# Attention and routed FFN: the slot rows' fill as eleven transfers beside the score tiles in place of four in a row

## The chip, the cores and the metric

The kernel runs on one core of a Trainium2 chip. A core has a matmul engine (TensorE, PE; its weight load is PEld), VectorE (DVE), ScalarE (ACT), GpSimd (POOL), SyncE (SP), which does nothing here but issue DMA transfers, and 16 DMA engines that all queues share. The metric is the device time of one execution in microseconds (us), taken as the median of several runs. A profile of one more execution gives the trace that is read below.

## The reference

Four sequences of 1024 rows of width 128 go through four residual blocks, each behind a layer norm:

```
x = x + attention_a(layernorm(x))      # 8 heads of 128, softmax(Q K^T + relative positions) V
x = x + ffn(layernorm(x))              # 8 experts, top 2 of each row
x = x + attention_b(layernorm(x))      # 16 heads of 8, causal
x = x + ffn(layernorm(x))

attn_pos = relative_shift(einsum(Q + rel_pos_bias, rel_k))   # row i of the product shifted by i
a = softmax(attn + attn_pos);  out = einsum(a, V) @ w_out + b_out

h = x W1[e]^T + b1[e];  g = h[:256] * sigmoid(h[256:])
out += (g Wo^T + bo) * share[e]         # for the two experts of each row
```

All is fp32. The weights and products that need it are split into a high and a low part, and a product is three matmuls.

## The kernel before

**Order of the work.** Three lists of steps (plans) are made in Python, and each engine walks through the same list and emits its share of each step. Plan 0 is attention_a, which takes about the first 1,600 us; plan 1 is the first FFN and attention_b; plan 2 the last FFN. What follows here is plan 0 (`plan_a`, from line 113).

**The score tiles.** The 256 tiles (4 sequences x 8 heads x 8 tiles of 128 query rows) are numbered 0 to 255, and step s of the plan works on tile s. Four tiles are a group (qd), 64 groups in all. For the relative positions, a strip of the position product is made three tiles ahead: TensorE multiplies (L1049, L1050), ScalarE and VectorE copy the result to `a_rt` (L1361 and L1798), SyncE stores it to DRAM (`rout`, L698, scr<-a_rt, 576 KB) and reads it back two tiles ahead with a row stride that is one element short, which makes the shift (`rin`, L707, a_sp<-scr, 512 KB). `a_rt` has two buffers, so ScalarE's copy for tile t waits for the store of tile t - 2 to have landed; the store and the load of neighbouring tiles are issued one behind the other. Then VectorE adds the scores of tile s to the strip and finds the maximum (L1806; one per tile, it waits for the load and for TensorE's L478 to L480), ScalarE takes the exponential (L1369), TensorE transposes (L1075), ScalarE and VectorE split the result (L1376, L1812), and TensorE multiplies by V (L1088 to L1090). When a group's product is done, ScalarE copies it out (L1382, a_osh) and raises the semaphore `o_hi` by one; group qd is copied in step 4 qd + 8.

**The slot rows.** The FFN is routed. Each row of x is scattered to the slots of its two experts in three arrays in DRAM, `xsd[0..2]`, one for each part of the sequences, with 39, 23 and 23 tiles of 128 rows (`PT[0]`). Slots that no row takes must hold finite numbers, so all the arrays are first filled with rows of the input q. This is the fill: DRAM to DRAM, issued by POOL (L785), 5.57 MB in all, in four transfers of 2048, 448, 1472 and 1472 KB. It is counted on the semaphore `d_zero`, together with the load of the output bias `fbo` (L787).

**POOL's list.** POOL runs its code in this order: the constants at the start; the expert weights W1 one by one (`w1` steps of the plan, at s = 52, 54, ... 68: L773 and L632 load 256 and 254 KB to SBUF, L781 subtracts, ScalarE and VectorE split the result, the semaphore `w1_lo` counts them); the fill; then, behind a wait for the last `w1_lo`, `fbo` and four constants (L788 to L794) that the ranking matmuls use; then the scatters of the first two parts (`m_disp`, L850), of which the first waits for `d_zero`. VectorE's `m_bias` step waits for `d_zero` too.

Of the kernel before, what the change touches and what calls it, by code (L numbers as in the profile page):

```python
# [16 lines left out]
B, L, D = 4, 1024, 128  # L17
# [25 lines left out]
PT = [[2 * L // 128 * len(p) + E - 1 for p in parts] for parts in PARTS]  # L43
PG = [[(t + 3) // 4 for t in row] for row in PT]
PP = [[(t + 1) // 2 for t in row] for row in PT]
MT = PT[0][0] + 1

ROWS = list(range(NT)), [n for k in range(8) for n in (3 * k, 3 * k + 1, 3 * k + 2, 24 + k)]
SC = float(DK) ** -0.5
# [438 lines left out]
class Program:  # L488
# [269 lines left out]
    def gpsimd(self, e):  # L758
        S = self.S
        cond = dict(pattern=[[-1, 128]], channel_multiplier=1, base=0)  # L760
        e.memset(self.ident[:, :], 0.0).then_inc(S["const"], 1)
        e.wait_ge(S["const"], 1)
        e.affine_select(out=self.ident[:, :], in_=self.ident[:, :], compare_op=ALU.not_equal, fill=1.0,
                        **cond).then_inc(S["const"], 1)
        e.iota(self.iota[:, :], pattern=[[1, E]], base=0, channel_multiplier=0,
               allow_small_or_imprecise_dtypes=True).then_inc(S["const"], 1)
        w1 = self.dr["w1t"].rearrange("d (e h) -> d e h", e=E)
        e.wait_ge(S["prod_mm"], H)
        for k in range(-1, E):
            if k > 0:  # L770
                e.wait_ge(S["w1_lo"], k)
            if k + 1 < E:
                e.dma_start(self.w1st[:, (k + 1) % 2, :], w1[:, k + 1, :]).then_inc(self.d_w1[(k + 1) % 2], 16)  # L773
                self.bottom_row(e, self.w1r[:, (k + 1) % 2, :], "w1r", self.d_w1[(k + 1) % 2], slice(512 * k + 512, 512 * k + 1024))
            else:
                e.dma_start(self.w1st[:, 0, 0:256].rearrange("p (k d) -> p k d", k=2),
                            self.dr["wo_f"].rearrange("(k p) d -> p k d", p=128)).then_inc(S["d_wo"], 16)
            if k >= 0:
                st = self.w1st[:, k % 2, :]
                e.wait_ge(self.d_w1[k % 2], 48 * (k // 2 + 1))  # L780
                e.tensor_tensor(st, st, self.w1r[:, k % 2, :], ALU.subtract).then_inc(S["w1_sub"], 1)  # L781

        for i, n0, n in ((0, 0, B * L), (0, B * L, PT[0][0] * 128 - B * L), (1, 0, PT[0][1] * 128), (2, 0, PT[0][2] * 128)):
            e.dma_start(self.xsd[i][n0:n0 + n, :], self.dr["q"][0:n, :]).then_inc(S["d_zero"], 16)  # L785
        e.wait_ge(S["w1_lo"], E + 1)
        e.dma_start(self.fbo[:, :], bass.AP(self.dr["bo_f"].tensor, 0, [[0, 128], [1, 128]])).then_inc(S["d_zero"], 16)  # L787
        e.memset(self.ones[:, :], 1.0).then_inc(S["m_const"], 1)  # L788
        e.wait_ge(S["m_const"], 1)
        e.affine_select(out=self.upper[:, :], in_=self.ones[:, :], compare_op=ALU.is_gt, fill=0.0, pattern=[[1, 128]],  # L790
                        channel_multiplier=-1, base=0).then_inc(S["m_const"], 1)
        e.iota(self.tio[:, :], pattern=[[1, MT]], base=0, channel_multiplier=0,
               allow_small_or_imprecise_dtypes=True).then_inc(S["m_const"], 1)
        e.iota(self.j128[:, :], pattern=[[128, 16]], base=0, channel_multiplier=0,  # L794
               allow_small_or_imprecise_dtypes=True).then_inc(S["m_const"], 1)
        for u in self.plans[0]:
            if u[0] == "m_disp":
                self.gpsimd_routed(e, u)

        self.first_attention_done(e)  # L800
        nst = 0
        for u in self.plans[1]:
            if u[0] == "b_s":
                _, b, g, ch, J, q = u
                pt, nst = nst % NP, nst + 1
                if J >= 4 * ch:
                    off = 128 * (J - 4 * ch)
                    e.wait_ge(S["b_exp"], nst)
                    e.affine_select(out=self.P[:, pt, off:off + 128], in_=self.P[:, pt, off:off + 128],  # L809
                                    compare_op=ALU.is_ge, fill=0.0, pattern=[[1, 128]], channel_multiplier=-1,  # L810
                                    base=0).then_inc(S["b_masked"], 1)
            elif u[0] == "b_load":
                dr = self.dr
                e.dma_start(self.pst, dr["w_b"].rearrange("d (k n) -> d k n", k=6)).then_inc(S["d_wb"], 16)
                e.dma_start(self.wvst[:, :], dr["wv_b"]).then_inc(S["d_wb"], 16)
                e.dma_start(self.bq[:, :], dr["bias_b"]).then_inc(S["d_wb"], 16)
                e.dma_start(self.bvo[:, :], bass.AP(dr["bvo_b"].tensor, 0, [[0, 128], [1, 136]])).then_inc(S["d_wb"], 16)
                e.memset(self.maskq[:, :], 0.0).then_inc(S["const"], 1)
                e.wait_ge(S["const"], 4)
                e.affine_select(out=self.maskq[:, 384:512], in_=self.maskq[:, 384:512], compare_op=ALU.is_ge, fill=NEG,  # L820
                                **cond).then_inc(S["const"], 1)
            elif u[0] == "b_zero":
                if u[1]:
                    e.wait_ge(S["m_ftr"], NT)
                    e.wait_ge(S["m_pmm"], NT)
                e.memset(self.K[u[1]][:, :, :].bitcast(F32), 0.0).then_inc(S["const"], 1)
            else:
                self.gpsimd_routed(e, u)
        for u in self.plans[2]:
            self.gpsimd_routed(e, u)  # L830

    def gpsimd_routed(self, e, u):
        S = self.S
        if u[0] == "m_disp":
            _, f, n = u
            i, part = 24 * f + n, part_of(f, n)
            if i == 0:
                e.wait_ge(S["d_zero"], 80)
            if n == 8 * PARTS[f][part][0]:
                e.wait_ge(S["m_slot"], 3 * f + part + 1)  # L840
                if f:
                    e.wait_ge(S["m_tr"], at(PG, 0, part + 1))
            if part == 2:
                rows, sem = self.xn8[:, n - 24, :], self.d_scat_last
                e.wait_ge(S["ln_xn"], 2 * ln_rank(2 * f + 1, B - 1) + 2)
            else:
                rows, sem = self.xd[:, i % 2, :], self.d_scat[i % 2]
                e.wait_ge(S["m_xd"], i + 1)
            for k in range(2):
                e.indirect_dma_start(self.xsd[part], bass.IndirectOffsetOnAxis(self.slot[:, k, n:n + 1], 0), rows,  # L850
                                     None).then_inc(sem, 16)
        elif u[0] == "m_gath":
            _, f, n = u
            i, part = NT * f + n, part_of(f, n)
            if n == 8 * PARTS[f][part][0]:
                end = at(PP, f, part + 1)
                for p in range(end - 4, end):
                    e.wait_ge(self.d_gs[p % 4], 16 * (p // 4 + 1))
            if i == 0:
                e.wait_ge(S["b_wlo"], 1)  # L860
            if i >= NP:
                e.wait_ge(S["m_sum"], rank(*divmod(i - NP, NT)) + 1 if n >= NP or f == 0 else NT)
            for k in range(2):
                e.indirect_dma_start(self.gb[:, i % NP, k, :], None, self.gsd[part],
                                     bass.IndirectOffsetOnAxis(self.slot[:, k, n:n + 1], 0)).then_inc(self.d_gath[i % NP], 16)
# [702 lines left out]
    def vector_routed(self, e, u):  # L1568
        S, ps, x = self.S, self.ps, self.x
# [4 lines left out]
        elif u[0] == "m_slot":  # L1574
            _, f, part = u
            tmp, le, bs = self.tmp, self.le, PARTS[f][part]
            n0, nb, nt = 8 * bs[0], len(bs), 8 * len(bs)
# [36 lines left out]
            for k in range(2):  # L1614
                for b in bs:
                    c0 = 8 * nt * k + 64 * (b - bs[0])
                    i = e.tensor_tensor(tmp[:, c0:c0 + 64].rearrange("p (n e) -> p n e", e=E), self.hot[:, k, 8 * b:8 * b + 8, :],
                                        self.rk[:, b, 0:64].rearrange("p (n e) -> p n e", e=E), ALU.mult)
# [5 lines left out]
        elif u[0] == "m_disp":  # L1624
            _, f, n = u
            i, b = 24 * f + n, n // 8
# [6 lines left out]
        elif u[0] == "m_bias":  # L1633
            _, f, b = u
            if f == 0 and b == 0:
                e.wait_ge(S["d_zero"], 80)
            if b < B - 1:
                e.wait_ge(S["m_xd"], 24 * f + 8 * b + 8)
            else:
# [1 line left out]
            for n in range(8 * b, 8 * b + 8):  # L1641
                i = e.scalar_tensor_tensor(x[:, n, :], self.fbo[:, :], self.csum[:, n:n + 1], x[:, n, :], ALU.mult, ALU.add)
            self.step(i)
        elif u[0] == "m_turn":
            _, f, part, g, bank = u
            i, w = at(PG, f, part) + g, 128 * min(4, PT[f][part] - 4 * g)
# [3 lines left out]
        elif u[0] == "m_mm":  # L1650
            _, f, part, n, bank = u
            i, k = at(PP, f, part) + n, min(2, PT[f][part] - 2 * n)
# [390 lines left out]
```

## Time and profile before

| | |
|---|---|
| median of 3 runs | 2677.7 us (2677.33 to 2683.09) |
| the profiled execution's own time | 2668.37 us |
| its span, first to last instruction | 2666.4 us |
| TensorE busy | 2444.4 us, 92% of the span |
| VectorE, ScalarE, GpSimd busy | 72%, 58%, 15% |
| mean granted TensorE clock | 0.948 |
| DMA traffic | 394.84 MB, mean 148 GB/s |

The profiled execution is one single run; its time stands beside its span, since the rows of the profile are in the span's time. Busy shares are means over stages that are bound differently. The profile also gives each engine's busy tenths in 40 slices of the span (66.7 us each), the chain of work that ended last, the waits (who stood idle until whom), the timeline, and the busy time of each engine in stretches that one may choose.

### The profile page before, as it was taken

What the parts mean: (1) busy time and instruction counts of PE and PEld (TensorE: products, weight loads), DVE (VectorE), ACT (ScalarE), POOL (GpSimd) and SP (SyncE); (2) the same over time, 40 slices, a digit from 0 to 9 for tenths busy, and PEclk for the clock granted to TensorE, in tenths of its full rate; (3) what the DMA queues carried; (4) which work ended last, traced back from release to release, by engine and by line L of the source; (5) the groups of instructions that cost most, each with busy time, mean ns of one, the idle gap of its engine ahead of it and who ended that gap; (6) DMA issues with size and microseconds to landing.
All of it is one profiled execution on the core that took longest, in us unless ns stands there. A gap on an engine that the chain in (4) does not pass through costs nothing.

```text
span 2666.4 us, 40535 instructions
## 1 busy us (share of the span) xinstructions
PE 2444.4 (92%) x13322; PEld 1884.1 (71%) x13322; DVE 1922.2 (72%) x4785; ACT 1553.9 (58%) x3113; POOL 410.6 (15%) x793
## 2 busy tenths in 40 slices
PE   4999898999999999999999977889999989988788
PEld 3788787888888888888888855665555545554566
DVE  4677776777877778777777754588877877874567
ACT  3566665666766666666566633537666656655333
POOL 0000011000000012000020005522222223414042
PEclk8999999999999999999999987779999989998889
DMA  4766578666666567666577625500000000000342
GB/s 135 237 232 222 184 257 288 215 206 223 231 223 231 205 217 244 212 231 218 201 242 242 225 88 170 153 20 1 1 1 1 1 5 11 18 11 16 93 142 68
DMA packets 164098, 394.84 MB, mean 148 GB/s; under 512 B 27426, under 2 KB 78498, under 8 KB 163554
## 3 DMA queue, kind: packets, MB, share of 16 engines
q1 hardware_dynamic: 148402, 355.85, 39.7%
q0 software_dynamic: 10928, 32.47, 4.0%
q10 hardware_dynamic: 4560, 3.93, 0.5%
q8 instruction: 108, 1.77, 0.3%
q14 instruction: 100, 0.82, 0.1%
HBM read 205.27 MB, written 189.60 MB: 148 GB/s over the span
## 4 chain that ended last, share of the span: by engine, by line
PE 76%; DVE 12%; ACT 5%; issue 5%; DMA 2%; POOL 1%; SPq 0%; another core or an unknown queue 0%; DVEq 0%; ACTq 0%; POOLq 0%
PE ps L478 8%; PE ps L480 8%; PE ps L479 8%; PE ps L1075 7%; PE ps L1187 5%; PE ps L1148 5%; PE ps L1050 5%; PE ps L1049 5%; PE ps L1169 4%; PE ps L1088 4%; PE ps L1090 4%; PE ps L1089 4%; DVE ps L1904 2%; PE ps L952 1%; DVE r_mx L1908 1%
## 5 line engine op out<-in xcount | busy, mean ns | idle before, releaser
L1376 ACT ACTIVATE a_Ph<-ps 128x512 fp32r<-128x512 f32 x512 | 305.2, 596 | 439.9 <-PE ps L1075 435.5
L1425 ACT ACTIVATE r_P<-ps 128x512 f32<-128x512 f32 (+3 forms) x768 | 329.9, 492 | 199.5 <-PE ps L1169 175.9
L1806 DVE CUSTOM_DVE_ANT_0 a_sp<-ps,a_sp 128x1024 f32<-128x1024 f32 x256 | 313.0, 1223 | 144.6 <-PE ps L480 123.0
L1812 DVE TENSOR_TENSOR a_Pl<-ps,a_Ph 128x512 fp32r<-128x512 f32 x512 | 348.9, 682 | 9.5 <-ACT a_Ph L1376 9.5
L1049 PE MATMUL ps<-a_fa,a_ua 128*128 128x384 f32 (+2 forms) x960 | 327.0, 353 | 21.8 <-ACT a_rt L1361 19.4
L1369 ACT ACTIVATE a_sp<-a_sp,a_nm 128x1024 f32<-128x1024 f32 x256 | 295.0, 1152 | 49.6 <-DVE a_nm L1806 48.9
L1075 PE MATMUL ps<-ident,a_sp 128*128 128x128 f32 x2048 | 308.0, 273 | 0.0
L1148 PE MATMUL ps<-r_K,r_Q 128*128 128x512 f32 (+3 forms) x768 | 281.9, 408 | 28.5 <-DVE r_mx L1904 14.8
L1075 PEld LDWEIGHTS ps<-ident,a_sp 128*128 128x128 f32 x2048 | 257.0, 141 | 70.7 <-issue 1.0
L1050 PE MATMUL ps<-a_fb,a_ub 86*128 86x384 f32 (+2 forms) x960 | 290.5, 317 | 0.0
L1904 DVE CUSTOM_DVE_ANT_0 ps<-ps,r_maskq 128x256 f32<-128x256 f32 (+3 forms) x512 | 244.2, 503 | 39.9 <-PE ps L1148 37.7
L1361 ACT ACTIVATE a_rt<-ps 128x384 f32<-128x384 f32 x512 | 251.1, 490 | 25.4 <-DMA scr<-a_rt 13.7
L1169 PE MATMUL ps<-r_Q,r_K 128*128 128x512 f32 (+3 forms) x768 | 253.5, 386 | 8.2 <-ACT r_P L1425 6.2
L1148 PEld LDWEIGHTS ps<-r_K,r_Q 128*128 128x128 f32 x768 | 146.2, 199 | 146.1 <-DVE r_mx L1904 74.6
L1088 PE MATMUL ps<-a_Ph,a_nath 128*128 128x512 f32 x512 | 214.9, 420 | 26.9 <-DVE a_Pl L1812 26.8
L850 POOL DMA_INDIRECT xsd<-m_xd,m_slot x96 | 95.7, 997 | 899.6 <-issue 505.8
L809 POOL TENSOR_SCALAR_AFFINE_SELECT r_P<-r_P 128x128 f32<-128x128 f32 x512 | 152.9, 310 | 425.6 <-ACT r_P L1425 417.5
L478 PE MATMUL ps<-p_xh,a_gah 128*128 128x512 f32 x512 | 208.3, 407 | 2.2 <-DVE a_ub L1780 1.6
L480 PE MATMUL ps<-p_xh,a_gal 128*128 128x512 f32 x512 | 206.0, 402 | 0.0
L1169 PEld LDWEIGHTS ps<-r_Q,r_K 128*128 128x128 f32 x768 | 143.0, 200 | 88.8 <-ACT r_P L1425 63.6
L1049 PEld LDWEIGHTS ps<-a_fa,a_ua 128*128 128x128 f32 x960 | 184.1, 192 | 30.2 <-ACT a_rt L1361 23.5
L479 PE MATMUL ps<-p_xl,a_gah 128*128 128x512 f32 x512 | 205.4, 401 | 0.0
(262 smaller groups left out, 4970.1 us busy)
## 6 DMA issues: line engine op xcount, KB each, us to landing
scr<-a_rt SPq DMA_DIRECT2D x256, 576.0 KB
a_sp<-scr SPq DMA_DIRECT2D x256, 512.0 KB, 4.5
gsd<-m_gg SPq DMA_DIRECT2D x71, 256.0 KB
a_share<-rdr SPq DMA_DIRECT2D x64, 256.0 KB, 4.6
a_wc<-wsp SPq DMA_DIRECT2D x24, 512.0 KB, 5.6
m_sx<-xsd SPq DMA_DIRECT2D x33, 256.0 KB
wsp<-a_wc SPq DMA_DIRECT2D x8, 512.0 KB, 5.5
xsd<-in_q POOLq DMA_DIRECT2D x2, 1472.0 KB, 19.3
```

Of the source, the lines that this page charges most:

```text
L478: e.matmul(out, lh, rh, start=True, stop=False)
L479: e.matmul(out, lh, rl, start=False, stop=False)
L480: return e.matmul(out, ll, rh, start=False, stop=True)
L1049: e.matmul(out, self.ua[:, s, side, qs], self.fa[:, base + a:base + z], start=True, stop=False)
L1050: i = e.matmul(out, self.ub[:, s, side, qs], self.fb[:, base + a:base + z], start=False, stop=True)
L1075: i = e.transpose(ps[:, 4 + j % 2, 128 * k:128 * k + 128], self.sp[:, (4 * qd + k) % NSP, 128 * j:128 * j + 128], ident[:, :])
L1088: e.matmul(OB, self.nath[:, s, j, :], self.Ph[:, slot, :], start=j == 0, stop=False)
L1148: e.matmul(ps[:, bank, 0:w], self.Q[b % 2][:, g, 128 * I:128 * I + 128], self.K[b % 2][:, q, 512 * part:512 * part + w], start=True, stop= ...
L1169: e.matmul(ps[:, bank, off:512], self.K[b % 2][:, q, 128 * J:128 * J + 128], self.Q[b % 2][:, g, 512 * ch + off:512 * ch + 512], start=Tru ...
L1425: e.activation(self.P[:, pt, off:512], ps[:, bank, off:512], ACT.Exp).then_inc(S["b_exp"], 1)
L1806: e.tensor_tensor_reduce(out=w, in0=ps[:, 2:4, :].rearrange("p a n -> p (a n)"), in1=w, scale=-1.0, scalar=3e38, op0=ALU.add, op1=ALU.min, ...
L1812: e.tensor_tensor(self.Pl[:, n % 2, :], ps[:, 4 + n % 2, :], self.Ph[:, n % 2, :].bitcast(F32), ALU.subtract).then_inc(S["p_lo"], 1)
```

## The change

The four transfers of the fill become eleven of at most 1024 rows (512 KB; the last of each array has 896 rows, 448 KB). They stand on POOL behind `fbo` and the constants, and each waits for a count of `o_hi`: the first for 18, the next for 19, and so on to 28. As `o_hi` rises once for each group of four tiles, one transfer goes out with each group from the eighteenth on. The waits for `d_zero` are for twelve transfers in place of five.

```diff
+FILLS = [(i, n, min(1024, 128 * t - n)) for i, t in enumerate(PT[0]) for n in range(0, 128 * t, 1024)]
...
-        for i, n0, n in ((0, 0, B * L), (0, B * L, PT[0][0] * 128 - B * L), (1, 0, PT[0][1] * 128), (2, 0, PT[0][2] * 128)):
-            e.dma_start(self.xsd[i][n0:n0 + n, :], self.dr["q"][0:n, :]).then_inc(S["d_zero"], 16)
         e.wait_ge(S["w1_lo"], E + 1)
         e.dma_start(self.fbo[:, :], bass.AP(self.dr["bo_f"].tensor, 0, [[0, 128], [1, 128]])).then_inc(S["d_zero"], 16)
...
+        for k, (i, n0, n) in enumerate(FILLS):
+            e.wait_ge(S["o_hi"], 18 + k)
+            e.dma_start(self.xsd[i][n0:n0 + n, :], self.dr["q"][0:n, :]).then_inc(S["d_zero"], 16)
         for u in self.plans[0]:
             if u[0] == "m_disp":
                 self.gpsimd_routed(e, u)
...
             if i == 0:
-                e.wait_ge(S["d_zero"], 80)
+                e.wait_ge(S["d_zero"], 16 * len(FILLS) + 16)
...
             if f == 0 and b == 0:
-                e.wait_ge(S["d_zero"], 80)
+                e.wait_ge(S["d_zero"], 16 * len(FILLS) + 16)
```

In POOL's list of instructions, from the last W1 subtraction on, this stood in a row before (names are output<-input, then the shape in elements; each "waits" names the semaphores):

```order
L781 TENSOR_TENSOR a_w1st<-a_w1st,a_w1r 128x512 [waits d_w1_1]
L785 DMA xsd<-in_q 32x16384
L785 DMA xsd<-in_q 16x7168
L785 DMA xsd<-in_q 32x11776 x2
L787 DMA m_fbo<-in_bo_f 128x128 [waits w1_lo]
L788 MEMSET m_ones 128x128
L790 AFFINE_SELECT m_upper<-m_ones 128x128 [waits m_const]
L792 IOTA m_tio 128x40
L794 IOTA m_j 128x16
L850 DMA xsd<-m_xd,m_slot 4992x128 [waits m_xd,m_slot,d_zero]
L850 DMA xsd<-m_xd,m_slot 4992x128
```

and this stands there now:

```order
L783 TENSOR_TENSOR a_w1st<-a_w1st,a_w1r 128x512 [waits d_w1_1]
L786 DMA m_fbo<-in_bo_f 128x128 [waits w1_lo]
L787 MEMSET m_ones 128x128
L789 AFFINE_SELECT m_upper<-m_ones 128x128 [waits m_const]
L791 IOTA m_tio 128x40
L793 IOTA m_j 128x16
L799 DMA xsd<-in_q 16x8192 [waits o_hi] x4
L799 DMA xsd<-in_q 16x7168 [waits o_hi]
L799 DMA xsd<-in_q 16x8192 [waits o_hi] x2
L799 DMA xsd<-in_q 16x7168 [waits o_hi]
L799 DMA xsd<-in_q 16x8192 [waits o_hi] x2
L799 DMA xsd<-in_q 16x7168 [waits o_hi]
```

The fill has moved from ahead of `fbo` to behind the constants, each of its transfers has a wait of its own, and its pieces are 8192 or 7168 elements long where they were up to 16384. The lists of the other four engines hold the same instructions in the same order.

## Rows read from the trace of the kernel before

**Rows 1.** The page: TensorE busy, slices, DMA rate, chain by engine

```profile
PE 2444.4 (92%) x13322; PEld 1884.1 (71%) x13322; DVE 1922.2 (72%) x4785; ACT 1553.9 (58%) x3113; POOL 410.6 (15%) x793
...
PE   4999898999999999999999977889999989988788
...
GB/s 135 237 232 222 184 257 288 215 206 223 231 223 231 205 217 244 212 231 218 201 242 242 225 88 170 153 20 1 1 1 1 1 5 11 18 11 16 93 142 68
...
PE 76%; DVE 12%; ACT 5%; issue 5%; DMA 2%; POOL 1%; SPq 0%; another core or an unknown queue 0%; DVEq 0%; ACTq 0%; POOLq 0%
```

**Rows 2.** Stretches: us, PE, PEld, DVE, ACT, POOL busy (instructions), clock, DMA share, GB/s

```profile
454.00:456.00 2.00, 0.87 (x6) 0.50 (x4) 0.00 (x0) 0.00 (x0) 0.00 (x0) 1.00 1.39 510
...
464.00:466.00 2.00, 0.00 (x0) 0.00 (x0) 0.00 (x0) 0.00 (x0) 0.00 (x0) 0.50 0.74 208
```

**Rows 3.** The waits from 443 to 475: who waited for whom, total, times, longest

```profile
DVE a_sp L1806 <- DMA a_sp<-scr: 15.8, 1, 15.8
ACT a_rt L1361 <- DMA scr<-a_rt: 13.2, 1, 13.2
...
PE ps L1049 <- ACT a_rt L1361: 11.9, 1, 11.9
```

**Rows 4.** Timeline of SyncE's queue: start, us, engine, line, what

```profile
445.06 0.32 SPq L698 DMA_DIRECT2D scr<-a_rt  x1
445.47 0.60 SPq L707 DMA_DIRECT2D a_sp<-scr  x1
```

**Rows 5.** Timeline of POOL, with the idle time before and its releaser

```profile
443.61 1.99 POOL L785 DMA_DIRECT2D xsd<-in_q  x4
480.11 0.57 POOL L787 DMA_DIRECT2D m_fbo<-in_bo_f  x1 [34.51 <-DVE wol L1762]
...
969.51 1.08 POOL L850 DMA_INDIRECT xsd<-m_xd,m_slot  x1 [488.02 <-issue]
```

**Rows 6.** The fill's line: duration in ns, first and last start; time to landing

```profile
L785 POOL DMA_DIRECT2D xsd<-in_q x4: 491/496/528, 443.6 to 445.1; - x4
...
DMA to landing us min/median/max: 11.3/15.0/21.2
```

**Rows 7.** DMA by queue, 445 to 452, then 452 to 467: packets, MB, share

```profile
q0 software_dynamic: 30, 1.90, 98.7%
...
q0 software_dynamic: 144, 3.47, 65.7%
```

**Rows 8.** Stretches of nine strides with the fill, and 64 tiles later without

```profile
446.51:513.55 67.04, 53.37 (x283) 44.95 (x282) 39.86 (x81) 34.33 (x66) 1.30 (x5) 0.90 0.74 246
828.24:878.90 50.66, 50.64 (x283) 43.27 (x282) 38.85 (x78) 33.38 (x64) 0.00 (x0) 1.00 0.67 225
```

**Rows 9.** The strips' load, L707, from 590 to 760: time to landing

```profile
DMA to landing us min/median/max: 4.2/5.2/5.8
```

**Rows 10.** Timeline of SyncE and VectorE at one tight load

```profile
594.36 0.37 SPq L707 DMA_DIRECT2D a_sp<-scr  x1
...
600.72 1.23 DVE L1806 CUSTOM_DVE_ANT_0 a_sp<-ps,a_sp 128x1024 f32<-128x1024 f32 x1 [0.40 <-PE ps L480]
```

**Rows 11.** The waits from 590 to 754: VectorE's score step

```profile
DVE a_sp L1806 <- PE ps L480: 15.3, 20, 1.7
```

**Rows 12.** ScalarE's copy of osh, which raises o_hi: count, first and last start

```profile
L1382 ACT ACTIVATE a_osh<-ps x11: 597/597/598, 520.4 to 752.2; 128x512 fp32r<-128x512 f32 x11
```

**Rows 13.** The W1 loads of 256 KB, L773, from 340 to 350: landing

```profile
DMA to landing us min/median/max: 5.7/6.0/6.3
```

**Rows 14.** Stretches of 20 us: beside the W1 loads, and about 540

```profile
346.00:366.00 20.00, 20.00 (x111) 17.20 (x110) 16.41 (x27) 13.00 (x25) 4.77 (x7) 1.00 0.91 294
520.00:540.00 20.00, 18.95 (x107) 15.87 (x106) 16.54 (x34) 12.76 (x26) 0.00 (x0) 1.00 0.67 229
540.00:560.00 20.00, 19.98 (x111) 17.09 (x111) 12.67 (x44) 9.57 (x19) 0.00 (x0) 0.91 0.51 173
```

**Rows 15.** The weight loads of 64 KB, L642, from 50 to 400: landing

```profile
DMA to landing us min/median/max: 1.9/2.4/3.1
```

## The prediction

> **What bounds the kernel now.** The page comes first. TensorE is busy for 92% of the span and holds 76% of the chain that ended last; DMA holds 2% of it [rows 1]. The slices of 67 us show one exception inside the first attention: in the seventh slice (400 to 467 us) PE drops to 8 where its neighbours have 9, and the DMA rate is at its highest, 288 GB/s. The stretches of 2 us open that slice [rows 2]. PE has 0.87 us of work in 454 to 456 and none from there to 466, by when the clock is at half (1.2 in place of 2.4 GHz). Who ended the idle time is in the waits [rows 3]: ScalarE's strip copy waited 13.2 us for a store of a_rt to DRAM, VectorE 15.8 us for the a_sp load, and TensorE 11.9 us for that ScalarE copy. The reader should compare this with the load's landing time in the rest of the stage, 4.2 to 5.8 us [rows 9].
>
> What held the load? POOL issued the four fills from 443.61 on, in 1.99 us [rows 5], and SyncE issued store and load at 445.06 and 445.47, behind them [rows 4]. The fills landed 11.3 to 21.2 us after issue; the last was issued at 445.1, so the fill ended near 466.3 [rows 6], and VectorE's step followed the load at 467.5. By queue, only POOL's queue (q0) moves data from 445 to 452, and from 452 to 467 it still has 65.7% of the engines [rows 7]. So the stall is the fill's transfers, standing ahead of the strips.
>
> **What the stall costs.** It is more than TensorE's idle time, since the clock falls as well. I compare nine strides of the score tiles here (the tenth a_sp step starts at 513.55) with the same nine strides 64 tiles later. Both stretches hold 283 matmuls. They take 67.04 and 50.66 us [rows 8], a difference of **16.4 us**. The second has mean clock 1.00 and PE 50.64 of 50.66 busy: it is what is left when the fill doesn't stand in the way.
>
> **The change, part by part.**
> 1. Four fills removed from 443.6: gain 16.4 us. TensorE works without a gap on both sides of the hole, and every later stage starts from what it ends, so I carry all of it to the end. What is late next? Nothing in that window: in the reference stretch the engine is full.
> 2. The wait for the last split weight, the load of fbo and four small constants now stand ahead of the fills on POOL. Before, fbo was issued at 480.11, after 34.5 us of waiting [rows 5]; it still waits for the same VectorE step, which comes some 16 us earlier. Cost nothing: nobody waits for them before the rank matmuls some 80 us on.
> 3. Eleven waits on o_hi. Queued behind them on POOL is only the first scatter, at 969.5 [rows 5]. The eleven copies of osh that release them start from 520.4 to 752.2 [rows 12], and 16 us earlier after the change, so the last fill is out over 200 us before that scatter. VectorE's bias step waits for the fills too, later still. Cost nothing; the cover is those 200 us.
> 4. Seven more issues on POOL. An issue takes 0.49 to 0.53 us [rows 6]; POOL stands idle for 488 us ahead of the first scatter in any case [rows 5]. Cost nothing.
> 5. The same 5.57 MB now go out in eleven pieces of 512 KB (448 KB three times), each beside running strips. This is the unknown. Before, 5.57 MB held the engines for 22.7 us (443.6 to 466.3), so one 512 KB fill holds them for 22.7 x 0.524/5.57 = 2.1 us (an estimate). The shares of the rest: DMA is busy for 0.67 of the reference stretch [rows 8], which leaves a third of each stride of 5.5 us, 1.8 us, unused; a fill every 22 us takes a tenth. So bandwidth is there, and only the delay of one load counts. The tightest I found: a load issued at 594.36, on a stretch where they land in 4.2 to 5.8 us, is there by 600.2 at the latest [rows 9, 10], and VectorE takes it at 600.72, when it had waited 0.40 us for TensorE and not for the load [rows 10]. The slack is 0.5 us by that bound, 1.3 us by the median of 5.2, say 0.9 us. The eleven copies of osh stand 23 us apart on average, which puts one at about 597: its fill would go out in the middle of that load. Delayed by a whole 2.1 us the load would be 1.2 us late, and eleven times that is **13 us, the upper end**. The **lower end is 0**: where a load comes before the time at which it is used, nobody waits. Below nothing it doesn't go, since outside the hole TensorE has no wait for a strip to give back.
>
> Which end? The nearest row is the w1 loads at 346 to 349: four transfers of 255 KB in the same POOL queue within 3 us, twice the bytes of a fill. The two of the weight itself landed in 5.7 to 6.3 us [rows 13] with DMA at 0.91 and 294 GB/s for 20 us, and TensorE was busy for 20.00 of 20.00 us [rows 14]. They write to SBUF in short pieces, a fill copies DRAM to DRAM in pieces of 32 KB (16x8192 elements in the order), so I don't take zero but 1 us for all eleven.
>
> Is there a fixed cost for each transfer? A weight load of 64 KB lands 1.9 to 3.1 us after issue [rows 15], though it has an eighth of the bytes of a fill; that part doesn't shrink with size. But in this trace it is not time in which the engines are held. A store of 576 KB and a load of 512 KB are issued together in each stride, and the load lands in 5.2 us: the bytes of both take 3.8 us at 294 GB/s, and two times 2.1 us of held engines on top would be 8.0. So it is latency, and nobody is behind a fill to feel it: 0. The Trainium skill has a rule that speaks against this change: "DMA: Bandwidth & Descriptors", section "Anatomy of one DMA — SWDGE (gpsimd) path", gives each transfer a fixed 2.0 us besides its bytes at 436 GB/s, and if one counted that as cost, seven more transfers would take back 14 us, an estimate from that page, and leave a gain of 2.4 us instead of the 15.4 below.
>
> Sum: 16.4 - 1 = **15.4 us less**. The profiled execution itself took 2668.4 us (span 2666.4) and would take 2653.0; the median of the runs is 9.3 us above it, and I put the same difference on it: 2677.7 - 15.4 = **2662.3 us**.
>
> **The rivals.**
> - *Part of the stall comes back in small change* (0.09). Each fill makes one load late by up to 1.2 us: 16.4 - 13 = 3.4 us gain at worst, 2674. For it: strips have under 1 us of slack in places, and the hole itself shows how a fill delays a load. Against: the w1 row, and VectorE has idle time before most a_sp steps, so part of a delay is caught up.
> - *The fixed part counts* (0.03). If every transfer held its engines for 2.1 us besides its bytes, seven more would take 14.7 us, gain 1.7, 2676. Against: the pair of store and load above, which would land at 8 us and lands at 5.2.
> - *Slower* (0.04). The 32 KB pieces get ahead of the store and the load of a stride, TensorE pauses, and the clock falls as after the hole. A short pause is enough for that: in 520 to 540 PE was idle 1.05 us, and the stretch behind it has clock 0.91 with PE full, where 0.09 x 20 = 1.8 us of it are lost [rows 14]. With 1.2 us exposed and 1.8 us of clock, 3.0 us for each fill, 33 in all: 2677.7 + 16.6 = 2694. It decides from 16.4 / 11 = 1.5 us per fill. Against: from 590 to 754 VectorE's a_sp steps waited for TensorE alone [rows 11].
> - *It doesn't do what it says* (0.02): the hole stays because something else shut q1 out. The order shows the fills gone from there, and nothing else in q0 remains at 443, so: 2677.7.
>
> **How the numbers follow.** The forecast has 0.82: own range 2659 to 2667 (0 to 4 us of cost, and runs that differ by a few us). 0.2%, about 5.4 us, is what a measurement of this kernel can tell from no change. Faster by more than that: 0.82 and two thirds of the first rival, 0.88. Within it: the last third, the fixed part and the last rival, 0.03 + 0.03 + 0.02 = 0.08. Slower: 0.04. The range of 8 in 10 is 2655 to 2671: below, the profiled runs lie under the median; above, half of the first rival.
>
> **What would show it.** In the changed profile: no a_sp load over 8 us; the nine strides from the same tile in about 51 us with 283 matmuls at clock 1.00; eleven fills from about 504 to 736 us, landing in 4 to 7 us; DMA between them under 0.8; TensorE's waits from 500 to 740 no longer than before by over 1 us. I am wrong if VectorE's a_sp step or ScalarE's strip copy shows waits for DMA behind each fill, or if the clock falls there.

## The result, and the profile after

The changed kernel takes 2660.1 us (median of 11 runs, 2645.9 to 2666.0) against 2677.3 us of the kernel before (11 runs, 2664.0 to 2684.1): a ratio of 0.9942, 95% interval 0.9921 to 0.9963, or 15.5 us less (10 to 21). A second chip, on which both kernels are some 43 us faster, gave 2616.1 against 2634.0 us, ratio 0.9945 (0.9928 to 0.9962). The forecast was 2662.3 us, 15.4 less. The profiled execution took 2655.9 us, its span is 2653.9 us.

The page of the changed kernel, the lines that answer to [rows 1]:

```profile
PE 2444.2 (92%) x13322; PEld 1884.6 (71%) x13322; DVE 1923.4 (72%) x4785; ACT 1553.5 (59%) x3113; POOL 415.5 (16%) x800
...
PE   4999899999999999999999977889999989988788
...
GB/s 143 234 233 225 185 257 257 224 231 246 252 232 229 195 231 223 224 232 212 209 239 241 217 78 184 137 12 1 1 1 1 1 7 10 18 11 14 95 142 68
...
PE 75%; DVE 12%; ACT 5%; issue 5%; another core or an unknown queue 1%; POOL 1%; DMA 1%; SPq 0%; DVEq 0%; ACTq 0%; POOLq 0%
```

TensorE's busy time is that of before to 0.2 us, 2444.2 against 2444.4. The seventh slice has its 9, and DMA's share of the chain has gone from 2% to 1%. The 288 GB/s of that slice are spread: it has 257, and the five slices behind it have 224 to 252 where they had 206 to 231.

The stretches of the changed kernel: the nine strides from the same tile on (compare [rows 8]), and the 55 strides behind them, in which the fills now go out; columns as in [rows 2]:

```profile
444.17:494.81 50.64, 50.62 (x283) 43.25 (x282) 39.88 (x80) 34.20 (x66) 1.29 (x5) 1.00 0.68 226
494.81:811.08 316.27, 314.64 (x1742) 269.87 (x1740) 237.58 (x461) 205.01 (x399) 5.44 (x11) 0.99 0.71 237
```

and the same 55 strides of the kernel before, without a fill in them:

```profile
513.55:828.24 314.69, 313.09 (x1739) 268.27 (x1738) 237.21 (x460) 204.93 (x399) 0.00 (x0) 0.99 0.65 221
```

The nine strides went from 67.04 to 50.64 us, **16.4 us less**, and the stretch that took over the fills is 1.6 us longer (DMA 0.71 in place of 0.65). The last of the 256 score tiles has its a_sp step at 1530.11 us in place of 1545.76, 15.6 us earlier. Before and after, up to the first of the nine strides, from the 55 strides to that last tile, and from there to the end:

```profile
0.00:446.51 446.51, 394.20 (x2082) 331.94 (x2083) 315.96 (x653) 268.13 (x504) 27.04 (x44) 0.97 0.66 219
828.24:1545.76 717.52, 706.08 (x3911) 603.44 (x3910) 547.93 (x1092) 457.03 (x888) 46.62 (x48) 1.00 0.66 223
1545.76:2666.40 1120.64, 977.70 (x5315) 635.51 (x5313) 781.25 (x2501) 589.47 (x1257) 335.68 (x696) 0.90 0.15 46
```

```profile
0.00:444.17 444.17, 391.93 (x2082) 330.22 (x2083) 315.90 (x653) 268.08 (x504) 25.17 (x40) 0.97 0.65 219
811.08:1530.11 719.03, 707.37 (x3910) 604.45 (x3908) 548.34 (x1091) 457.14 (x888) 46.71 (x48) 0.99 0.66 222
1530.11:2653.90 1123.79, 979.65 (x5315) 636.85 (x5313) 781.71 (x2501) 589.10 (x1257) 336.87 (x696) 0.90 0.15 46
```

In these three stretches both kernels run the same code. The first is 2.3 us shorter in the changed kernel, the second 1.5 us longer and the third 3.1 us longer.

Who waited, in the changed kernel, from 500 to 740 us (where all fills lie); of TensorE's and VectorE's waits, the groups that could be the fill's:

```profile
POOL xsd L799 <- ACT a_osh L1386: 267.9, 11, 39.6
...
DVE a_sp L1810 <- PE ps L482: 18.8, 23, 2.5
...
PE ps L1092 <- DVE a_Pl L1816: 0.7, 1, 0.7
...
PE ps L925 <- DVE a_gal L1789: 0.5, 1, 0.5
DVE a_sp L1810 <- issue: 0.5, 1, 0.5
...
PE ps L894 <- DVE a_gal L1789: 0.4, 1, 0.4
```

TensorE's three pauses of 0.7, 0.5 and 0.4 us stand in the kernel before at the same steps, with 0.6, 0.5 and 0.4 us. No row names a DMA; the one of 0.5 us that names "issue" has no releaser in the trace and is probably a load, as the wait of 13.1 us under that name at e9's stall is (below). The only engine that waits for long is POOL, for the copies of osh, as it should. The fills and the strips' load there (L799 and L709):

```profile
L799 POOL DMA_DIRECT2D xsd<-in_q x11: 488/488/534, 502.6 to 735.8; - x11
...
DMA to landing us min/median/max: 3.5/4.4/7.1
```

```profile
DMA to landing us min/median/max: 4.1/4.5/5.4
```

The load landed in 4.1 to 5.4 us beside the fills, no later than the 4.2 to 5.8 us without them [rows 9]. These two traces hold the landing of only 10 of 42 and 11 of 30 loads. A second profile of the changed kernel (e6 below) has it of all 41 from 500 to 740 us:

```profile
DMA to landing us min/median/max: 3.9/4.8/5.8
```

In e4 below, which has no fill in that stretch, all 41 landed in 4.1 to 6.1 us, median 4.6.

### The profile page after: what moved, and what is told of

Its sections match the earlier page's. It is cut to its first block, busy times and chain, and to the rows that moved or that the text cites. A ratio compares the mean times of both kernels' runs of the same rounds, so it can differ in the third digit from the quotient of the medians.

```text
span 2653.9 us, 40542 instructions
## 1 busy us (share of the span) xinstructions
PE 2444.2 (92%) x13322; PEld 1884.6 (71%) x13322; DVE 1923.4 (72%) x4785; ACT 1553.5 (59%) x3113; POOL 415.5 (16%) x800
## 4 chain that ended last, share of the span: by engine, by line
PE 75%; DVE 12%; ACT 5%; issue 5%; another core or an unknown queue 1%; POOL 1%; DMA 1%; SPq 0%; DVEq 0%; ACTq 0%; POOLq 0%
PE ps L480 8%; PE ps L482 8%; PE ps L1079 8%; PE ps L481 8%; PE ps L1152 5%; PE ps L1191 5%; PE ps L1054 5%; PE ps L1053 5%; PE ps L1173 5%; PE ps L1092 4%; PE ps L1094 4%; PE ps L1093 4%; DVE ps L1908 2%; DVE r_mx L1912 1%
## 5 line engine op out<-in xcount | busy, mean ns | idle before, releaser
L1810 DVE CUSTOM_DVE_ANT_0 a_sp<-ps,a_sp 128x1024 f32<-128x1024 f32 x256 | 313.2, 1223 | 127.0 <-PE ps L482 120.3
L1094 PE MATMUL ps<-a_Ph,a_natl 128*128 128x512 f32 x512 | 203.0, 396 | 0.0
L1093 PE MATMUL ps<-a_Pl,a_nath 128*128 128x512 f32 x512 | 201.8, 394 | 0.0
```

Source lines behind the costliest of these rows:

```text
L1810: e.tensor_tensor_reduce(out=w, in0=ps[:, 2:4, :].rearrange("p a n -> p (a n)"), in1=w, scale=-1.0, scalar=3e38, op0=ALU.add, op1=ALU.min, ...
```

## The experiments

All theories are about one question: what about the fill shut the strips out? **A**: the bytes that come at once, against the third of the DMA engines that each stride leaves free and a slack of about 1 us. **B**: the length of a piece, 64 KB. **C**: that transfers were issued in a row. And there is the new place, away from the W1 steps. Each run was timed beside the kernel before on its own chip, e1, e2, e4 and e5 on one, e6 to e9 on another, so runs are compared through their ratios. Stretches are cut at the same tiles as above: nine strides, then 55.

### e1: eleven pieces, in a row, at the old place

```diff
+        for k, (i, n0, n) in enumerate(FILLS):
+            e.dma_start(self.xsd[i][n0:n0 + n, :], self.dr["q"][0:n, :]).then_inc(S["d_zero"], 16)
         e.wait_ge(S["w1_lo"], E + 1)
...
-        for k, (i, n0, n) in enumerate(FILLS):
-            e.wait_ge(S["o_hi"], 18 + k)
-            e.dma_start(self.xsd[i][n0:n0 + n, :], self.dr["q"][0:n, :]).then_inc(S["d_zero"], 16)
```

> The eleven pieces of the change, issued without waits at the old place (behind the last W1 subtraction). Theory A (it is the backlog of bytes that stands ahead of the strips): the hole comes back, TensorE is idle for 10 us or more, the nine strides take 63 to 67 us as before, and the time is that of the kernel before within 4 us. Theory B (it is the size of a single piece, 64 KB before and 32 KB here): the hole shrinks to half or less, the nine strides take 51 to 58 us, and at least 8 us of the gain stay.

2631.5 against 2631.8 us, ratio 1.0005 (0.9987 to 1.0022): the whole gain is gone. The nine strides, and the waits from 443 to 480, with the columns of [rows 3]:

```profile
445.52:513.71 68.19, 53.71 (x283) 45.19 (x282) 39.85 (x80) 34.29 (x66) 3.72 (x11) 0.87 0.72 247
```

```profile
DVE a_sp L1809 <- DMA a_sp<-scr: 16.6, 1, 16.6
ACT a_sp L1372 <- DVE a_nm L1809: 8.1, 1, 8.1
ACT a_rt L1364 <- DMA scr<-a_rt: 8.0, 1, 8.0
...
PE ps L1091 <- DVE a_Pl L1815: 7.5, 1, 7.5
```

68.19 us where the kernel before has 67.04. Halving the pieces won nothing back. A holds; B, in the form that 32 KB pieces share better, falls.

### e4: the four old transfers in pieces of 4 KB

```diff
+        for i, n0, n in ((0, 0, B * L), (0, B * L, PT[0][0] * 128 - B * L), (1, 0, PT[0][1] * 128), (2, 0, PT[0][2] * 128)):
+            to = self.xsd[i][n0:n0 + n, :].rearrange("(a b) d -> a (b d)", b=8)
+            e.dma_start(to, bass.AP(self.dr["q"].tensor, 0, [[0, n // 8], [1, 1024]])).then_inc(S["d_zero"], 16)
         e.wait_ge(S["w1_lo"], E + 1)
```

(in place of the change's loop; every eight slot rows get the same first eight rows of q)

> The four transfers at the old place and in a row, but in pieces of 4 KB in place of up to 64 KB (the same 4 KB of q repeated as the source). The bytes written are those of before; the bytes read come from 4 KB. Theory A (backlog of bytes): the hole is as before, 13 us of idle TensorE, a strip's load lands 20 us after issue. 
2632.0 against 2631.8 us, ratio 1.0005 (0.9984 to 1.0026). The nine strides:

```profile
442.70:510.95 68.25, 55.66 (x283) 46.46 (x282) 39.85 (x80) 34.40 (x66) 2.48 (x7) 0.90 0.84 253
```

From 440 to 460 us SyncE's queue (q1) has 35.3% of the engines, but that mean hides two phases. DMA by queue from 441 to 448, and then from 448 to 459 us (columns as in [rows 7]):

```profile
q0 software_dynamic: 291, 1.19, 84.5%
q1 hardware_dynamic: 1, 0.00, 0.2%
```

```profile
q1 hardware_dynamic: 481, 1.61, 52.7%
q0 software_dynamic: 365, 1.36, 44.8%
```

and in the kernel before, from 452 to 463:

```profile
q0 software_dynamic: 126, 3.38, 86.9%
q1 hardware_dynamic: 126, 0.58, 13.0%
```

The first phase is no better than before: SyncE issued a store at 441.24 and its queue moved its first packet 6.7 us later; in the kernel before that was 7.6 us, with 32 KB pieces (e1) 5.4 us, and for stores away from the fill 0.3 to 0.8 us. So the 7 us in which SyncE's queue is shut out [rows 7] are not due to the length of a piece, and what they are due to stays open. The second phase is what B said: with 4 KB pieces SyncE's queue has half of the engines, where it had 13%. The strips' loads issued from 438 to 482 us landed in up to 15.1 us (median 10.9), between the 20 us of A and the 8 to 12 of B. The waits from 438 to 482 us:

```profile
POOL xsd L787 <- issue: 18.5, 1, 18.5
...
PE ps L1092 <- DVE a_Pl L1816: 9.5, 2, 5.6
```

POOL did not issue its third transfer for 18.5 us, and waited for no semaphore meanwhile; a full queue is my reading of it, which no run tested. TensorE's longest wait is 5.6 us where it was 11.9. Yet the stall is no smaller: 17.6 us over the 50.66 without a fill. The turns decide who is served first; the bytes that must be moved before the strips catch up stay, and they cost the same in four pauses between 451 and 478 us as in one long hole (TensorE was idle 12.6 of the 68.25 us, and the clock was at 0.90). So the length of a piece is not the cause of the cost. One thing besides the length changed in this run: the third and fourth transfer went out 20 us after the first two.

### e9: the eleven at once, at the new place

```diff
-            e.wait_ge(S["o_hi"], 18 + k)
+            e.wait_ge(S["o_hi"], 18)
```

> The changed kernel with all eleven fills waiting for the same count of o_hi, 18: they go out in a row at about 503 us, where the changed kernel starts, and not beside the last W1 steps. It parts the new place from the spacing. Theory A (spacing is what gains): a hole of TensorE of 8 to 14 us appears at 510 to 530 us, the nine strides at 444 are 50.7 us, and the time is 0 to 6 us under the kernel before. Rival (the place is what gains, away from the W1 loads and splits): no hole over 3 us, the time of the changed kernel within 3 us.

2630.9 against 2634.0 us, ratio 0.9991 (0.9973 to 1.0009). The nine strides and the 55 behind:

```profile
446.69:497.34 50.65, 50.63 (x283) 43.25 (x282) 39.84 (x80) 34.18 (x66) 1.28 (x5) 1.00 0.67 226
497.34:826.38 329.04, 316.19 (x1739) 270.04 (x1738) 237.28 (x460) 204.79 (x399) 5.34 (x11) 0.97 0.66 228
```

The old place is clean, 50.65 us, and the stall stands at the new one, 329.04 us against 314.69 of the kernel before, or 16.1 us over the 312.9 that it takes at full clock without a stall (e4 and e8 below). VectorE's wait there:

```profile
DVE a_sp L1810 <- issue: 13.1, 1, 13.1
```

The wait for the count is there, the W1 steps are not: the place gains nothing that these runs can tell (the interval allows up to 7 us), the spacing gains the rest.

### e2: the four old transfers, spaced

```diff
-FILLS = [(i, n, min(1024, 128 * t - n)) for i, t in enumerate(PT[0]) for n in range(0, 128 * t, 1024)]
+FILLS = [(0, 0, B * L), (0, B * L, PT[0][0] * 128 - B * L), (1, 0, PT[0][1] * 128), (2, 0, PT[0][2] * 128)]
...
-            e.wait_ge(S["o_hi"], 18 + k)
+            e.wait_ge(S["o_hi"], 18 + 3 * k)
```

> The four transfers of before in their old sizes (2048, 448, 1472, 1472 KB), each alone, three groups of tiles apart. Theory A (backlog): a load behind 2048 KB is late by up to 8.4 us and one behind 1472 KB by up to 6.0, less 1 us of slack each: holes of 7, 5 and 5 us, 17 us in all, and the time is about that of the kernel before (2 to 17 us of the gain gone). Theory C (only transfers issued in a row hurt): no hole, the time is that of the changed kernel within 2 us.

2625.4 against 2631.8 us, ratio 0.9980 (0.9960 to 0.9999), so about a third of the gain (5 us, by the interval 0 to 11). C falls: a transfer that stands alone also makes a hole, when it is large. The 55 strides, and 20 us around the third transfer:

```profile
498.80:824.94 326.14, 317.72 (x1740) 271.44 (x1738) 237.57 (x460) 205.03 (x399) 2.04 (x4) 0.98 0.69 230
```

```profile
660.00:680.00 20.00, 16.75 (x76) 13.88 (x75) 10.81 (x25) 11.37 (x20) 0.00 (x0) 0.83 0.63 199
```

TensorE is idle for 8.4 of the 326.14 us, where before it was 1.6. That is 6.8 us of holes, and not the 17 us of the expectation: the strips' load was late by less than the bytes of the fill would give, as its landing times from 500 to 740 us show (5.5 us over the median at most, where 8.4 was expected):

```profile
DMA to landing us min/median/max: 4.1/5.2/10.7
```

The other half of the loss in this stretch is the clock: TensorE is busy for 317.72 us with the work that takes 311.3 at full clock (e4 and e8 below), 6.4 us more. Part of it stands in the row from 660 to 680 us, where a pause of over 3 us is followed by half clock (mean 0.83).

### e5, e7 and e8: how much at a time

e5 doubles the bytes with each group (`dup` is eleven spare arrays in DRAM), e7 makes a fill up to 1 MB, e8 makes them 256 KB:

```diff
+            e.dma_start(self.dup[k][0:n, :], self.dr["q"][0:n, :]).then_inc(S["d_zero"], 16)
```

```diff
-FILLS = [(i, n, min(1024, 128 * t - n)) for i, t in enumerate(PT[0]) for n in range(0, 128 * t, 1024)]
+FILLS = [(i, n, min(2048, 128 * t - n)) for i, t in enumerate(PT[0]) for n in range(0, 128 * t, 2048)]
```

```diff
-FILLS = [(i, n, min(1024, 128 * t - n)) for i, t in enumerate(PT[0]) for n in range(0, 128 * t, 1024)]
+FILLS = [(i, n, min(512, 128 * t - n)) for i, t in enumerate(PT[0]) for n in range(0, 128 * t, 512)]
...
-            e.wait_ge(S["o_hi"], 18 + k)
+            e.wait_ge(S["p_exp"], 77 + 2 * k)
```

> The changed kernel with each fill followed at once by a copy of the same size to a spare array: 1 MB with each group in place of 512 KB, 22 transfers. It doubles the suspected cost of one fill. Forecast by slack: a load is late by up to 4.2 us against about 1 us of slack, so up to 3 us for each group, 5 to 30 us in all. Rival (a fill costs nothing whatever its size, since TensorE is never waiting for strips in these groups): the time is that of the changed kernel within 2 us.

> The changed kernel with fills of up to 2048 rows (1 MB), seven transfers, one with each group from the eighteenth on. Theory A (what counts is how many bytes come at once against a slack of about 1 us and the idle third of each stride): like the doubled bytes of the run before, TensorE pauses of 0.3 to 1 us at the four whole ones, 1 to 4 us over the changed kernel. Rival (only the number of bytes in all counts): no difference from the changed kernel.

> The changed kernel with 22 fills of at most 512 rows (256 KB), one with every second tile from about the same place on. Theory A: nothing is left to win, since at 512 KB no load was late: the time is that of the changed kernel within 2 us. Rival (a fixed cost of each transfer counts): eleven more transfers cost 2 us each, 20 us in all. Second rival (fills of 512 KB still cost TensorE something through late loads): 2 to 5 us less than the changed kernel.

Beside them on e7's and e8's chip ran the changed kernel itself:

> The changed kernel once more, on the same chip as the next three. Both theories: 15 us (12 to 18) under the kernel before, nine strides of 50.7 us, TensorE's idle time between 440 and 760 us under 2.5 us.

| run | MB in fills, at a time | ratio to the kernel before (95%) | 55 strides | clock in them |
|---|---|---|---|---|
| e8 | 5.57, 256 KB | 0.9951 (0.9934 to 0.9967) | 312.89 us | 1.00 |
| e6, the change | 5.57, 512 KB | 0.9945 (0.9928 to 0.9962) | 317.66 us | 0.98 |
| e7 | 5.57, up to 1 MB | 0.9955 (0.9936 to 0.9974) | 317.06 us | 0.99 |
| e5 | twice 5.57, 1 MB | 0.9957 (0.9938 to 0.9976) | 319.55 us | 0.99 |

By the runs' times these four can't be told apart (their intervals reach 4 to 5 us to either side). e6 does what was expected of the change (14.5 us less by the ratio, nine strides of 50.65 us, 1.6 us of idle TensorE), and the rival of e8, 20 us of fixed costs, is refuted by its time alone. For the rest there are the profiles. First the 55 strides of e8, with 22 fills in them, and of e4, where no fill is left in this stretch:

```profile
495.05:807.94 312.89, 311.27 (x1739) 267.02 (x1738) 237.31 (x460) 204.93 (x399) 10.78 (x22) 1.00 0.73 240
```

```profile
510.95:823.91 312.96, 311.36 (x1739) 267.11 (x1738) 237.30 (x460) 204.82 (x399) 0.00 (x0) 1.00 0.65 222
```

312.89 with the fills, 312.96 without, and the same 1.6 us of idle TensorE in both. **In these profiles a fill that is small enough costs TensorE nothing**, and 22 issues cost no more than none. What makes e6 longer is the clock alone: its TensorE is idle for 1.6 us too (317.66 less 316.04). In e7 it is idle for 3.9 us (317.06 less 313.17), 2.3 of them in one pause at 592.3 us, behind a fill of 1 MB issued at 580 and a load that was issued at 583 and landed after 9.6 us. The expectation had a short pause at each of the four whole fills; only this one stands there. The same stretch of e5:

```profile
495.56:815.11 319.55, 314.30 (x1739) 267.98 (x1738) 237.44 (x461) 204.82 (x399) 10.69 (x22) 0.99 0.75 252
```

TensorE is idle for 5.3 us there, so 3.7 us for eleven doubled fills, in five pauses of 0.5 to 1.0 us: less than the 5 to 30 us that slack alone foretold, but not nothing. TensorE's idle time thus begins to grow between 512 KB and 1 MB with a group.

Whether the fills have a part in the lost clock, these profiles don't settle. With the same work TensorE is busy in the 55 strides for 311.3 us in e8 and 311.4 in e4, 312.9 and 313.1 in e1 and the kernel before (like e4 without a fill there), 313.2 in e7, 314.3 in e5, and 314.6 and 316.0 in the two profiles of the change. So e8's expected rival, that smaller fills save 2 to 5 us more, stays open for the clock: its stretch is 3.4 and 4.8 us shorter than those of the change, its time is not (2619.2 against 2616.1 us).

## Why the prediction was right

**What bounds and what the stall costs.** 16.4 us from the nine strides, and 16.4 us came. The stretch 64 tiles later was a good stand-in for what is left without the fill: it gave 50.66 and the stretch itself is now 50.64. TensorE's idle time alone (13.7 us) would have been too little; the rest is half clock behind the hole.

**The POOL steps, waits and issues at no cost.** fbo is issued at 461.6 in place of 480.1, and the first scatter starts at 953.6, 217 us after the last fill. These two rows of POOL's timeline show it:

```profile
735.78 0.49 POOL L799 DMA_DIRECT2D xsd<-in_q  x1 [21.52 <-ACT a_osh L1386]
953.60 1.06 POOL L854 DMA_INDIRECT xsd<-m_xd,m_slot  x1 [217.34 <-DVE m_xd L1635]
```

**The eleven fills, 1 us (0 to 13).** By TensorE's idle time it was 0: 1.6 us in the 55 strides after (316.27 less 314.64) as before (314.69 less 313.09). The choice of 1 us went by the w1 row, which pointed the right way without giving the reason, so that it came this near is in part luck. The step that was off is the sentence that a fill goes out in the middle of a load and delays it by up to 2.1 us. The 2 us stretches at that very load show why it doesn't. Before:

```profile
595.00:597.00 2.00, 2.00 (x15) 1.86 (x14) 1.29 (x3) 1.28 (x3) 0.00 (x0) 1.00 1.01 328
597.00:599.00 2.00, 2.00 (x13) 1.70 (x13) 1.75 (x4) 2.00 (x5) 0.00 (x0) 1.00 0.52 186
599.00:601.00 2.00, 2.00 (x13) 1.64 (x12) 1.60 (x4) 0.78 (x2) 0.00 (x0) 1.00 0.26 99
```

and after, for the same tile, with the fill issued at 580.00:

```profile
578.00:580.00 2.00, 2.00 (x15) 1.82 (x14) 1.47 (x3) 1.48 (x4) 0.00 (x0) 1.00 1.01 309
580.00:582.00 2.00, 2.00 (x13) 1.71 (x12) 1.75 (x4) 2.00 (x5) 0.49 (x1) 1.00 1.00 348
582.00:584.00 2.00, 2.00 (x13) 1.68 (x12) 1.60 (x4) 0.62 (x3) 0.00 (x0) 1.00 0.52 212
```

The engines are idle for half and then three quarters of the two stretches before the next store is issued, and the copy of osh releases the fill just there: 512 KB went into the hole. The load (issued at 594.36 before, 577.16 after) landed after 5.4 us in both, and VectorE's step again had 0.40 us of wait for TensorE before it. So the slack of about 0.9 us was right (it was 0.98), and the delay of 2.1 us did not come. I had the free third of a stride as a mean and did not look at where in the stride it lies. The place of 597 us for that fill came out right too (580.00 is 597.2 in the times of before), but not from the mean distance of 23 us, which gives 590. e8, whose release is another semaphore, meets loads more often, and still TensorE's idle time does not grow, since the slack takes it: its loads land in 4.1 to 6.7 us, median 5.3, where e6 has 4.8.

**The signs of being wrong.** One of them came up: the clock did fall between the fills, to 0.83 from 520 to 540 us (last section). No fill's wait stands ahead of it: TensorE's pauses before it are those of the kernel before. The fills landed in 3.5 to 7.1 us, a little outside the 4 to 7 given.

**The rivals.** The small change that comes back (up to 13 us) is 0 of TensorE's idle time at 512 KB, and e5 shows how it begins, at about 0.3 us a group when the bytes are doubled. The fixed part of a transfer is no cost: e8 has eleven transfers more than the change, by that rival 23 us, and its 55 strides are the shortest. With it falls the reading that was set against the change from the Trainium skill, "DMA: Bandwidth & Descriptors", section "Anatomy of one DMA — SWDGE (gpsimd) path"; its 2.0 us are time to landing, and nobody waited for a landing here. The slower case wanted 1.5 us for each fill; e2 shows its mechanism at work, pauses with half clock behind them, but with transfers of 1.5 and 2 MB. That the hole had another cause is refuted by e9, where it moves with the fills.

**The sum against the profile.** The profiled pair differs by 12.5 us and not 15.4. The nine strides give 16.4. Another 2.3 us come from ahead of them, where the same 2082 matmuls kept TensorE busy for 391.93 in place of 394.20 us. Lost again are 1.6 us in the 55 strides, which is clock (no TensorE pause more than before, but 0.83 of full clock from 520 to 540 us), 1.5 us from there to the last score tile, of which 1.3 are TensorE's busy time again, and 3.1 us behind that tile. The terms of 1.5 to 3.1 us stand where both kernels run the same code, and single executions differ there by some us: the first of the nine strides starts at 446.51 us in the kernel before, at 444.17 in the changed one and at 446.01 in e6. Why the last stretch took 3.1 us more stays open. The prediction carried the 16.4 us to the end, and this pair can show that only to some 3 us. The medians, 17.2 and 17.9 us by plain difference and 15.5 and 14.5 by the ratios, sit on both sides of the forecast; the interval of 10 to 21 us does not confirm it to the microsecond.

## What to carry to other kernels

A bulk transfer that nobody is waiting for still costs time when it is issued at once beside a stream with little slack: what counts is the backlog it leaves against the idle share of the engines and the slack of the stream, and neither shorter pieces nor another place change that sum. Cut it so that one portion fits the idle time within a stride or two (here 512 KB, an estimated 2.1 us of the engines, where a stride of 5.5 us leaves 1.8), and release each portion by a semaphore of the stream itself, which also puts it at a fixed phase of the stride. To size the gain, compare the stalled stretch with the same steps of a later round: it counts the lost clock as well, which the idle time alone leaves out.

## What the runs showed of the hardware

When the fill of the kernel before was issued, SyncE's queue moved nothing for 7 us though it had work [rows 7], and 4 KB pieces did not shorten that by more than a microsecond (6.7 us from the store's issue to its first packet in e4, 7.6 before). Only behind that does the length of a piece set the share: 52.7% for SyncE's queue with 4 KB pieces against 13.0% with pieces of up to 64 KB. It does not set the length of the stall, 17.6 us in e4 against 16.4 before. The second phase agrees with the Trainium skill, "DMA: Bandwidth & Descriptors", section "Queues, rings and completion order" (each engine goes round the queues a packet at a time), if a long piece is one packet. Whether the first phase does is not shown by any run here.

TensorE's clock fell to half also where only short pauses stood before it. In each kernel with spaced fills it pauses for 0.6 to 0.7 and 0.4 us near 505 us, at a step where it waits for VectorE; so does the kernel before, at 523 us. From 520 to 540 us it is then busy throughout, at full clock in e8 and at a mean of 0.83 in the changed kernel, which gets 104 matmuls done in place of 121:

```profile
520.00:540.00 20.00, 19.98 (x121) 17.35 (x120) 14.24 (x47) 10.73 (x21) 0.49 (x1) 1.00 0.66 217
```

```profile
520.00:540.00 20.00, 19.98 (x104) 17.32 (x103) 11.21 (x28) 10.01 (x20) 0.52 (x1) 0.83 0.59 192
```

The 55 strides thus take 312.9 us at full clock and 316.3 and 317.7 us in the two profiles of the changed kernel, all with 1.6 us of idle TensorE. That is more than any idle time that the fills of the change cost, and it is one reason why single profiles of this kernel differ by some us.

The chips differ by more: the kernel before took 2677 us on the first and 2632 and 2634 us on the two others, three times the gain. Only ratios taken on one chip could show it. In the profiles the difference does not lie in the first attention: the changed kernel starts the a_sp step of its last score tile at 1530.1 us on the first chip and at 1532.0 on the other (e6), and takes 1123.8 and 1080.5 us from there to the end:

```profile
1532.04:2612.50 1080.46, 964.78 (x5315) 630.55 (x5313) 780.30 (x2501) 589.43 (x1257) 335.05 (x696) 0.92 0.16 47
```
